# A decoder layer on one core: the first attention's output bias moves to GpSimd, and the last batch's work stands in another order

## The reference, cut to what matters

```python
x = x + attn(layernorm(x))            # linear attention, 16 heads, with biases
x = x + xattn(layernorm(x), ctx, ctx) # cross attention with l2-normed q and k
x = x + ffn(layernorm(x))             # 8 experts, each token goes to its top 2

# attn
Q, K = elu(x@Wq.T + bq) + 1, elu(x@Wk.T + bk) + 1
V = x@Wv.T + bv
out = (Q @ (K^T V)) / (Q . sum(K) + 1e-6)
return out @ Wo.T + bo                # bo: the bias that this change moves
# ffn
out += gate[e] * (gelu(xn @ W1[e] + b1[e]) @ W2[e] + b2[e])   # for the two chosen e
```

## Time and profile before

| | us |
|---|---|
| median of 3 runs | 434.83 (433.38 to 438.06) |
| the profiled execution | 433.5 |
| its span | 431.6 |
| TensorE busy | 406.5 (94%) |
| VectorE busy | 342.7 (79%) |
| ScalarE busy | 304.7 (71%) |
| GpSimd busy | 247.9 (57%) |
| mean granted TensorE clock | 0.985 |

### The profile page before, as it was taken

One profiled execution on the slowest core, in us unless ns is written; L12 is line 12 of the kernel. 1 busy time (PEld: TensorE's weight loads), 2 busy tenths in 40 slices (PEclk: granted clock), 3 DMA queues, 4 the chain that ended last, 5 costly groups with the idle time before them and its releaser, 6 DMA issues.

```text
span 431.6 us, 8902 instructions
## 1 busy us (share of the span) xinstructions
PE 406.5 (94%) x3017; PEld 382.7 (89%) x3017; DVE 342.7 (79%) x836; ACT 304.7 (71%) x599; POOL 247.9 (57%) x350
## 2 busy tenths in 40 slices
PE   6998999999999999989999999999999999999970
PEld 6786898989989888978999999999999999999970
DVE  5645768778787899796778699979999899979950
ACT  3574566675756676456679888889889798889720
POOL 4444448485765784688664565535636686654331
PEclk9899999999999999999999999999999999999995
DMA  7901011203020522974599597996988899995531
GB/s 278 325 24 50 2 49 51 75 27 98 2 74 26 186 98 60 359 247 137 146 299 373 134 354 212 316 359 179 377 291 289 273 279 311 320 306 145 171 38 12
DMA packets 32194, 79.35 MB, mean 184 GB/s; under 512 B 4659, under 2 KB 23475, under 8 KB 26261
## 3 DMA queue, kind: packets, MB, share of 16 engines
q1 hardware_dynamic: 23184, 67.68, 44.1%
q0 software_dynamic: 7488, 10.39, 12.4%
q10 hardware_dynamic: 1476, 0.72, 0.6%
HBM read 69.14 MB, written 9.63 MB: 183 GB/s over the span
## 4 chain that ended last, share of the span: by engine, by line
PE 82%; DVE 10%; issue 2%; DMA 2%; ACT 2%; POOL 1%; SPq 0%; DVEq 0%; ACTq 0%; POOLq 0%
PE bank L433 61%; PE bank L440 4%; PE bank L900 4%; PE bank L669 2%; PE bank L742 2%; PE bank L651 2%; PE bank L881 1%; PE bank L721 1%; PE bank L751 1%; DMA aw_f<-aw_ 1%; DVE st L1358 1%; PE bank L702 1%; DVE w1l L1491 1%; DMA y_<-yb,idxs 1%; PE bank L601 1%
## 5 line engine op out<-in xcount | busy, mean ns | idle before, releaser
L2146 POOL DMA_INDIRECT y_<-yb,idxs x29 | 57.4, 1980 | 68.3 <-DMA y_<-yb,idxs 37.3
L433 PE MATMUL bank<-xh,w1h 128*128 128x256 f32 x256 | 74.6, 291 | 1.1 <-DVE xl L1768 1.0
L433 PE MATMUL bank<-w2h,hh 128*128 128x256 f32 x264 | 75.3, 285 | 0.0
L433 PE MATMUL bank<-w2l,hh 128*128 128x256 f32 x264 | 74.1, 281 | 0.0
L433 PE MATMUL bank<-w2h,hl 128*128 128x256 f32 x264 | 74.1, 280 | 0.0
L433 PE MATMUL bank<-xh,w1l 128*128 128x256 f32 x256 | 72.4, 283 | 0.0
L433 PE MATMUL bank<-xl,w1h 128*128 128x256 f32 x256 | 72.3, 283 | 0.0
L2084 POOL DMA_INDIRECT xg<-xn_rows,idxg x39 | 53.3, 1366 | 14.6 <-issue 10.5
L1491 DVE TENSOR_TENSOR w1l<-w1r,w1h 128x1024 fp32r<-128x1024 f32 x46 | 56.1, 1220 | 3.2 <-ACT w1h L1009 3.0
L433 PEld LDWEIGHTS bank<-xh,w1h 128*128 128x128 f32 x256 | 48.9, 191 | 1.9 <-issue 1.0
L433 PEld LDWEIGHTS bank<-w2l,hh 128*128 128x128 f32 x264 | 50.0, 189 | 0.0
(11 more groups left out here) (265 smaller groups left out, 1104.6 us busy)
## 6 DMA issues: line engine op xcount, KB each, us to landing
w1r<-ff_ SPq DMA_DIRECT2D x23, 1024.0 KB, 5.8
w2r<-ff_ SPq DMA_DIRECT2D x23, 1024.0 KB, 7.4
b1r<-b_ SPq DMA_DIRECT2D x7, 512.0 KB
bs<-ff_ SPq DMA_DIRECT2D x23, 132.0 KB, 5.5
xn_rows<-xn SPq DMA_DIRECT2D x8, 264.0 KB, 2.2
xin<-x_ SPq DMA_DIRECT2D x8, 256.0 KB, 6.7
cT<-ctxT_ SPq DMA_DIRECT2D x8, 256.0 KB, 4.8
cin<-ctx_ SPq DMA_DIRECT2D x8, 256.0 KB, 4.0
```

The source lines that it names most:

```text
L433: r = e.matmul(o, a_(t), b_(t), start=first and m == 0, stop=m == n - 1)
L2146: e.indirect_dma_start(out=out[:, :], out_offset=bass.IndirectOffsetOnAxis(ap=at, axis=0), in_=yb[t % 2][:, i, :], in_offset=None, compute ...
```

## The change: what it does

1. The bias of the first attention's output no longer comes from a matmul. A new tile `bo` gets it by a DMA to all 128 partitions, and `with_bias(s)` on GpSimd adds it in place to the input rows of batch `s` at the end of stage `s`, once the first norm has read them. `first(b)` waits for it, and so does `x_high(0)`, whose tile lies where `bo` lay. `biases()` works on 512 columns and not on 768.
2. `attention` is issued in two halves, and in stage 1 `norms(0)` stands between them.
3. In stage 7 and in the seam the calls stand in another order on TensorE, VectorE, ScalarE and GpSimd.

```diff
-                    e.matmul(o, one_r[:, 0:128], ab_r[:, 512:768], start=True, stop=False)
...
-                        last = e.matmul(o, aT[k][:, j, i * 128:(i + 1) * 128], awo_f[:, j, :], start=False, stop=j == 1)
+                        last = e.matmul(o, aT[k][:, j, i * 128:(i + 1) * 128], awo_f[:, j, :], start=j == 0, stop=j == 1)
...
+            e.dma_start(bo[:, :], ab[2 * D:3 * D].partition_broadcast(P)).then_inc(d_bo, 16)
...
+            def with_bias(b):
+                rows = xin[:, 2 * b:2 * b + 2, :]
+                if b == 0:
+                    e.wait_ge(d_bo, 16)
+                e.wait_ge(a_xln, 2 * b + 2)
+                e.tensor_tensor(rows, rows, rep(bo[:, :], 2), ALU.add).then_inc(g_xb, 1)
...
+                if s == NB - 1:
+                    ranks(s - 2)
+                with_bias(s)
...
             def first(b):
                 k = b % 2
                 e.wait_ge(p_x1, b + 1)
+                e.wait_ge(g_xb, b + 1)
...
             def x_high(t):
+                if t == 0:
+                    e.wait_ge(g_xb, NB)
```

TensorE, the loop and the list behind it:

```diff
-                if s >= 1:
+                if s >= 2:
                     norms(s - 1)
...
-                attention(s)
+                attention(s, 0)
+                if s == 1:
+                    norms(0)
+                attention(s, 1)
...
-                if s >= 2:
+                if 2 <= s < NB - 1:
                     rank(s - 2)
...
             attended(NB - 1)
-            count(NB - 3)
             xpose(0)
             projected(NB - 1)
+            rank(NB - 3)
             layer1(0, 0)
+            count(NB - 3)
+            layer1(0, 1)
+            xpose_2(NB - 1)
+            layer1(0, 2)
             invert(NB - 3)
             xpose_n(NB - 2)
-            layer1(0, 1)
-            layer1(0, 2)
-            xpose_2(NB - 1)
             layer1(0, 3)
```

VectorE, the list behind the loop (inside stage 7, `w1_low(0, 1)` now follows `w1_low(0, 0)`, and `add_inverse(4)`, `keep_count(1)`, `route_a(5)` follow `attention(7)`):

```diff
+            second(NB - 2)
+            x_split(0)
+            first(NB - 1)
             own_rank(NB - 3)
-            second(NB - 2)
             place_row(NB - 3)
-            x_split(0)
+            x1_normed(NB - 1)
             place_column(NB - 3)
             normed(NB - 2)
-            first(NB - 1)
+            x2T_low(NB - 1)
             add_inverse(NB - 3)
             keep_count(2)
-            early_expert(1)
-            x1_normed(NB - 1)
-            early_rows(1)
-            early_expert(2)
-            x2T_low(NB - 1)
-            early_rows(2)
-            early_expert(3)
+            early_tile(1)
+            early_tile(2)
             second_low(NB - 1)
-            early_rows(3)
             route_a(NB - 2)
+            early_tile(3)
             w1_low(1, 0)
-            early_tile(4)
+            w1_low(1, 1)
             own_rank(NB - 2)
-            w1_low(1, 1)
             x_split(1)
...
             add_inverse(NB - 2)
-            weigh(0, 1)
             x_split(2)
             w1_low(2, 1)
+            weigh(0, 1)
             route_a(NB - 1)
+            early_tile(4)
             w1_low(3, 0)
```

ScalarE and GpSimd, their lists behind the loop:

```diff
-            e.activation(gelu_at[:, :], eps[:, 2:3], ACT.Gelu_apprx_tanh)
             attended(NB - 1)
             x_affine(0)
             x_high(0)
-            xn_affine(NB - 2)
+            exponents(NB - 3)
+            e.activation(gelu_at[:, :], eps[:, 2:3], ACT.Gelu_apprx_tanh)
             gelu(0, 0)
             gelu(0, 1)
-            residual(NB - 2)
             x2T_high(NB - 1)
             gelu(0, 2)
+            xn_affine(NB - 2)
+            residual(NB - 2)
             gelu(0, 3)
...
+            norm_scale(NB - 2)
+            with_context(NB - 1)
+            scale_1(NB - 1)
+            residual_scale(NB - 2)
             gates(NB - 3)
-            norm_scale(NB - 2)
-            residual_scale(NB - 2)
             residual_factors(NB - 2)
-            scale_1(NB - 1)
             gather(1)
-            with_context(NB - 1)
             gather(2)
             ranks(NB - 2)
             scale_q(NB - 1)
             gather(3)
-            gather(4)
             norm_scale(NB - 1)
             exponents(NB - 2)
+            gather(4)
             gates(NB - 2)
```

More of the change, by code:

```diff
@@ L167, in decoder_layer @@
         qk_l0 = pa("qk_l0", [P, 2, 256], f32r)
-        pa("apart", [P, 1024])
+        bo = pa("bo", [P, D])
+        pa("apart", [P, 768])
         sqT = pa("sqT", [P, 2, 256])
@@ L297, in decoder_layer @@
         d_ct = [sem(f"d_ct{k}") for k in range(3)]
-        d_cs, d_cs2, d_aw, d_gb, d_ab, d_xw, d_wo, d_fc, d_wg, d_sp = (
-            sem(f"d_{n}") for n in ("cs", "cs2", "aw", "gb", "ab", "xw", "wo", "fc", "wg", "sp"))
+        d_cs, d_cs2, d_aw, d_gb, d_ab, d_xw, d_wo, d_fc, d_wg, d_sp, d_bo = (
+            sem(f"d_{n}") for n in ("cs", "cs2", "aw", "gb", "ab", "xw", "wo", "fc", "wg", "sp", "bo"))
         d_b = [sem(f"d_b{k}") for k in range(2)]
@@ L324, in decoder_layer @@
             sem(f"v_{n}") for n in ("x2Tl", "wkv", "qkl", "x2", "xn", "inv", "cnt"))
-        g_va, g_rs, g_cTl, g_xc, g_rb, g_rm = (sem(f"g_{n}") for n in ("va", "rs", "cTl", "xc", "rb", "rm"))
+        g_va, g_rs, g_cTl, g_xc, g_rb, g_rm, g_xb = (sem(f"g_{n}") for n in ("va", "rs", "cTl", "xc", "rb", "rm", "xb"))
         r_v, r_p, r_w, r_g, r_h, r_x, r_e, r_ex, r_cnt, r_invT, r_sel = (
@@ L733, in second_out, with attention @@
                           lambda t: fc_h[:, t, :], lambda t: fc_l[:, t, :], 2, True).then_inc(p_s7, 1)
-            def attention(s):
+            def attention(s, i):
                 n = s % 2
[L737 to L744, removed]
+                if i == 0:
+                    e.wait_ge(v_kvb, 2 * s + 2)
+                if i == 1 and s >= 1:
+                    e.wait_ge(a_sq7, 2 * s)
+                for m in range(2):
+                    last = e.matmul(banks[0 if i else 6][:, m * 136:(m + 1) * 136], phq[n][:, m, i * 128:(i + 1) * 128],
+                                    kvb[n][:, m, :], start=True, stop=True)
+                last.then_inc(p_at, 1)
             def context_sums(s):
@@ L931, in tensor @@
             invert(NB - 2)
+            layer1(1, 2)
             xpose_n(NB - 1)
-            layer1(1, 2)
             layer1(1, 3)
@@ L1170, in scalar @@
                     w1_high(0, 0)
+                    w1_high(0, 1)
                 squares_k(s)
@@ L1275, in scalar @@
             gelu(1, 0)
+            gelu(1, 1)
+            gelu(1, 2)
+            xn_affine(NB - 1)
             weigh(0, 1)
-            gelu(1, 1)
-            xn_affine(NB - 1)
-            gelu(1, 2)
             w1_high(3, 0)
@@ L1493, in biases @@
             def biases():
+                c = slice(0, 2 * D)
                 e.wait_ge(d_ab, 16)
@@ L1496, in biases @@
                 e.wait_ge(c_bias, 1)
-                e.tensor_copy(ab_h[:, :], ab_f[:, :]).then_inc(c_bias, 1)
+                e.tensor_copy(ab_h[:, c], ab_f[:, c]).then_inc(c_bias, 1)
                 e.wait_ge(c_bias, 2)
-                e.tensor_tensor(ab_f[:, :], ab_f[:, :], ab_h[:, :].bitcast(fp32), ALU.subtract).then_inc(c_bias, 1)
+                e.tensor_tensor(ab_f[:, c], ab_f[:, c], ab_h[:, c].bitcast(fp32), ALU.subtract).then_inc(c_bias, 1)
                 e.wait_ge(d_cs, 16)
                 e.wait_ge(c_bias, 3)
-                e.tensor_scalar(ab_t[:, :], ab_h[:, :].bitcast(fp32), const("m01")[:, 0:1], None,
+                e.tensor_scalar(ab_t[:, c], ab_h[:, c].bitcast(fp32), const("m01")[:, 0:1], None,
                                 ALU.mult).then_inc(c_bias, 1)
                 e.wait_ge(c_bias, 4)
-                e.scalar_tensor_tensor(ab_r[:, :], ab_f[:, :], const("m01")[:, 1:2], ab_t[:, :],
+                e.scalar_tensor_tensor(ab_r[:, c], ab_f[:, c], const("m01")[:, 1:2], ab_t[:, c],
                                        ALU.mult, ALU.add).then_inc(c_bias, 1)
@@ L1654, in vector, with older @@
                     x2T_low(0)
-                if s == NB - 1:
-                    w1_low(0, 0)
                 if s == 0:
                     xT_low(1)
-                if s >= 3:
-                    add_inverse(s - 3)
+                def older():
+                    if s >= 3:
+                        add_inverse(s - 3)
+                    if s >= NB - 2:
+                        keep_count(s - NB + 2)
+                    if s >= 2:
+                        route_a(s - 2)
                 if s == 1:
                     e.tensor_scalar(pr[:, :], const("iotae"), 8.0, None, ALU.mult).then_inc(r_e, 1)
[L1663 to L1667, removed]
+                if s < NB - 1:
+                    older()
+                else:
+                    w1_low(0, 0)
                     w1_low(0, 1)
@@ L1922, in decoder_layer @@
                     RS[_which, _b] = _n
-        for _which, _b in (("xn", NB - 2), ("y3", NB - 2), ("ln1", NB - 1), ("q", NB - 1), ("xn", NB - 1), ("y3", NB - 1)):
+        for _which, _b in (("xn", NB - 2), ("ln1", NB - 1), ("y3", NB - 2), ("q", NB - 1), ("xn", NB - 1), ("y3", NB - 1)):
             _n += 2
```

6 lines of the change are left out of this document (2 added, 4 removed).

## The result

| kernel | median us | lowest to highest | ratio to before, 95% |
|---|---|---|---|
| before | 435.38 (20 runs) | 432.77 to 439.77 | |
| the change | 437.50 (20 runs) | 435.51 to 510.04 | 1.0059, 1.0032 to 1.0087 |

On 435.4 us the ratio is 2.6 us, from 1.4 to 3.8. That is within the 1% that the prediction called "same" and the time is inside its range, but at its very end, and the interval does not hold 1: no change was forecast, and the change costs. (The ratio leaves the run of 510 us out, as a disturbed one.) The profiled execution took 436.09 us (span 433.8) against 433.5 (span 431.6).

What follows compares the result with a forecast made beforehand. TensorE was taken to bound the loop, with room only at the start and in the seam. A front gain of 2.0 us and a seam loss of 2.0 summed to 0: 433.5 us, own range 431.5 to 435.5, overall 428.8 to 437.5.

Steps and rivals of the forecast that it cites:

- the 1% that the prediction called "same": Whole kernel: measured time within about 1% (4.3 us) of no change, given a chance of 0.75.
- Front, -2.0: Start and loop: 1.4 us less from six batches' bias matmuls, 0.6 from an earlier start of TensorE.
- the second rival: Start: TensorE's clock does not fall after the shorter pause, saving the 1.7 us it cost: 431.8 us; chance 0.20.
- The added operation, 0: Loop: GpSimd's with_bias, 1.28 us eight times, falls in idle time and costs the stage 0.
- the rival of the lock in the loop: Loop: VectorE's reciprocal waits for with_bias, 0.67 us in each of seven stages: 438.2 us; chance 0.05.
- Stage 7, gain 0.5: Stage 7: kvb comes earlier, but the bias add takes back half; layer1(0, 0) at 164.7 where it was 165.19.
- Logits 2.4 earlier on top of the front: Seam: logits of batch 7 come 2.4 us earlier (1.5 to 3.3) as old waits go and new ones come.
- GpSimd, the gates 6.5 us behind the logits' end: Seam: gather(4), waiting for early_tile(4), delays batch 6's gates to 6.5 us behind the logits; GpSimd 5.0 us later.
- I take a loss of 2.0 us against now for the whole seam: Seam: GpSimd's lateness at batch 7's count and tile 5 costs 2.0 us net; bounds gain 3.3, loss 3.5.
- Gather of tile 5, 2.5 late: Tile 5: gather(5) lands at 234.4, 2.5 us late for TensorE's transposes; 1.7 if the first gather isn't stretched.
- the seam loses more: Seam: stretched gathers and tile 1's late landing add 3 us: 436.5 us; chance 0.10.

Runs made afterwards that it cites:

- e10: e3 with GpSimd's bias addition cut to one number, output lacking the bias; one profile: a stage of 18.86 us against 18.88.
- e3: The kernel before with the bias part alone, in the old order: 0.9912 of before, 431.5 us.
- e1: The changed kernel with gather(4) on GpSimd moved behind the gates of batch 6 and the ranks of batch 7: 0.9946 of before, 433.0 us.
- e2: The changed kernel with TensorE's pause at the count of batch 7 filled by 32 unused transposes: 1.0072 of before, 438.5 us.
- e12: e4 with gather(4) behind batch 7's ranks, gather(5) ahead of scatter(1, 0), scale_1(7) ahead of the context addition: 0.9957 of before, 433.5 us.
- e4: The kernel before with the new order alone, bias matmuls kept: 1.0029 of before, 436.6 us.
- e6: e1 with gather(5) also ahead of scatter(1, 0) on GpSimd: 0.9937 of before, 432.6 us.
- e8: e2 with gather(5) ahead of scatter(1, 0) on GpSimd: 1.0031 of before, 436.7 us.

## Why the prediction failed, point by point

1. **Front, -2.0: right in kind, too small.** A stage was to be 18.86 us; it is 18.9, with at most 0.02 for the addition. TensorE's first product was to come at 11.1 and came at 11.00. What I under-counted is the start behind it. TensorE's first product of batch 1 stands at 22.77 in the profile of before, and here in the changed kernel:

```profile
21.45 0.39 PE L434 MATMUL bank<-xT_h,aw_h 128*128 128x256 f32 x1 [0.52 <-DVE xT_l L1385]
```

   Of this 1.3 us, 0.7 is the earlier start; the rest is the clock (the second rival, true in this profile), less a new wait of 0.79 for `aw_l`, which the slow clock had hidden. From its first product to batch 1's it is 11.04 us before and 10.45 here, 9.66 without the new wait: the low clock had cost 1.4 us, where the rival had 1.7, and 0.8 of it came back as that wait.
2. **The added operation, 0: right.** e10 and the reciprocals of e3 show it, and the rival of the lock in the loop falls. That a VectorE instruction with at most one SBUF input does not contend with GpSimd (the Trainium skill, "SBUF — State Buffer", "Who interferes with whom") agrees with these rows: 0.25 us beside the addition and without it.
3. **Stage 7, gain 0.5: right in its mechanism.** `layer1(0, 0)` is at 162.05 with 1.14 us ahead of it for xl, 3.1 before its old 165.19; less the front's 2.6 that is the 0.5. ScalarE waited 0.95 us for `with_bias(7)`.
4. **Logits 2.4 earlier on top of the front: right in the sum by luck.** 195.31 less 4.4 was forecast, and 4.4 was measured. But the front gave 2.6 of it (batch 5's last norm is transposed at 145.76, before at 148.35), so the seam gave 1.8 and not 2.4.
5. **GpSimd, the gates 6.5 us behind the logits' end: right.** They begin at 198.34 behind logits that end at 191.93, 6.4. The count was forecast at 206.7 less the front's 2.0, 204.7; it is 204.74, by the same luck: it hangs on the logits.
6. **"I take a loss of 2.0 us against now for the whole seam": this step failed.** By the profiles the front is 2.6 us ahead and tile 6 is 2.0 behind (240.29 against 238.32), so the seam lost 4.6, not 2.0. The largest piece of the 2.6 between them is the low clock. The prediction let TensorE stand for 4 us at the count and go on at full rate; it went on at half rate, which cost 1.7 us in this profile and 1.3 to 2.8 over three. The price was in my own rows: I had worked out that a pause of 2.12 us at the start was followed by a low clock, and I asked only whether that one would go, not whether a pause twice as long that I was creating would bring another. Some 0.6 is the smaller gain up to the logits (point 4). Another 0.5 fell behind tile 5, where `x_affine(5)` ended 0.2 later behind the transposes than before and the cast to `xh` took 0.73 us in place of 0.43. Against these stand 0.3 that the prediction still lost between the count and tile 5.
7. **Gather of tile 5, 2.5 late: wrong.** The prediction carried GpSimd's 5.0 us on to `gather(5)`. GpSimd, before and in the changed kernel, ahead of `scatter(1, 0)`:

```profile
218.23 1.61 POOL L2146 DMA_INDIRECT y_<-yb,idxg  x1 [4.41 <-DVE idxs L1752]
```

```profile
219.38 1.61 POOL L2169 DMA_INDIRECT y_<-yb,idxg  x1 [2.46 <-DVE idxs L1768]
```

   Before, GpSimd idled there for 4.41 us, and this idle time took most of the lateness up. The gather's second DMA went out at 222.70, against 222.39 before and a forecast of 225.4 (227.4 less 2.0), and TensorE did not wait at tile 5. In e1 and e2 it did wait there, 2.41 and 2.10 us, but for a reason that the prediction does not have: `scatter(1, 0)`, ahead of the gather, stood for the landing of tile 0's scatters, in e1 with GpSimd not late at all. So with the pause taken out or filled, the next queue held.

The rival "the seam loses more" (0.10) came nearest in size, 436.5, but named stretched gathers and a late tile 1. What makes a wait dearer than its length was in none of my rivals.

## What to carry to other kernels

Where a change makes the busiest engine stand for several microseconds in one piece, price the pause at its length and the low clock behind it (here 4.1 and 1.3 to 2.8 us). A call that waits for late data must not stand in a queue ahead of calls whose data is there: `gather(4)` ahead of the gates, and `scatter(1, 0)` ahead of `gather(5)` in e1, held TensorE for 4.08 and 2.41 us, and moving one shows the next. Before a lateness is carried down a queue, subtract the idle time that the queue already has (4.41 us here). And measure the halves of a change apart: one gained 3.8 us here, and the other, on top of it, lost it all.

## What was unexpected of the hardware

- The low clock behind a 4.1 us pause varied between executions: 1.3, 1.7 and 2.8 us for the same work, each one a single profile.
- Behind shorter waits the clock fell in some profiles and not in others. At the start, a wait of 2.00 to 2.21 us was followed by the low clock in before, e12 and e1 (means of 0.66, 0.66 and 0.70 over 12 to 17 us) and not in e4 (1.00); one of 1.50 us in e6 (0.67) and in none of nine others. At tile 5, 2.10 us (e2) were followed by it and 2.41 (e1) were not. Kernels with the narrow bias operations mostly have the wait of 1.50, which may be part of why e3 gained 3.8 and not 2.0; too few profiles to say.
- With 32 transposes in place of the pause at the count the granted clock stayed at 1.00 there in both profiles (e2, e8), and the products behind them took their 3.62 us.
